# A branch prefetch hint at the head of each pass of the loops over row blocks in a three-layer graph network kernel

## The chip, the cores and the metric

The kernel runs on one core of one Trainium2 chip. The metric is the device time of one execution in microseconds; a kernel's time is the median of several executions.

## What is computed

`x` has 12,500 nodes of 64 features, `src` and `dst` list 412,500 edges. Three layers compute a gate for every edge and a gated, normalised sum over edges; a layer norm follows, then a plain degree-normalised sum with a dense product, and a second layer norm. Cut to what matters:

```python
for l in range(3):
    f1 = relu(x[row] @ nb_W[l] + nb_b[l]); f2 = relu(x[col] @ self_W[l] + self_b[l])
    h = relu(concatenate([f1, f2], axis=1) @ att1_W[l] + att1_b[l])
    mask = clip(sigmoid((h @ att2_W[l] + att2_b[l])[:, 0]) * 1.5 - 0.45, 0, 1)
    d = clip((segment_sum(mask, row) + 1e-6) ** -0.5, 0, 10)
    x = segment_sum((mask * d[row] * d[col])[:, None] * x[col], row)
    out = out + x
# then: layer norm; out = x + relu(segment_sum(x[col] * w, row) @ weight + bias); layer norm
```

## The kernel before

**Tiling.** The edges are sorted by row and column at the start (about the first 1.4 ms). Nodes form 98 blocks of 128 (`NB`), and all later edge work runs over the 98 blocks of rows, one after the other. Within a block of rows the edges lie in 51 tiles in 7 groups (`GROUPS`). Looking up `x[col]` and adding up per row are matrix products with one-hot matrices in fp8.

**Stages over row blocks.** There are seven such stages in an execution. Each of the three layers has an *edge stage*, which makes the gates (PE work: `cols` at L1033, `rows` at L1058, `row_sums` at L1083; in the first layer also `turn` at L1070, which transposes one-hots), and a *segment stage*, which sums the gated rows (PE work: `cols` at L1033, `scatter` at L1141). The seventh is the segment stage of the last graph layer. In the first edge stage DVE and ACT make the one-hots and SP stores them; in the others SP loads them.

**Engines.** Every engine (PE, DVE, ACT, POOL, SP) has its own instruction stream, and they meet only in semaphores. The order on each is the order in which it is written. A wait by `wait_alone` (L48) is an instruction of its own, EVENT_SEMAPHORE in the profile; L47 computes the value that it waits for, in a register.

**The loops.** A stage is written with `over_rows` (L415 and on): block 0 stands ahead of the loop in straight code, and a `Fori` of 97 passes does the other blocks. Its closing branch and its counter are recorded at L418, per pass one ALU_OP (counter + 1), one COMPARE_BRANCH (back to the head) and, at the head, one FUSED_REGOPS. PE, ACT and POOL use `over_rows` in all seven stages. DVE and SP use it in six: their part of the first edge stage is a `Fori` of its own, with 96 passes, outside `over_rows`. The stages of layers 2 and 3 stand once in the program, inside an outer loop over the layers.

Of the kernel before, what the change touches and what calls it, by code (L numbers as in the profile page):

```python
# [50 lines left out]
def gnn_kernel(nc, x, src, dst, nb_W, nb_b, self_W, self_b, att1_W, att1_b, att2_W, att2_b,  # L51
# [4 lines left out]
    NB = -(-N // P)  # L56
# [46 lines left out]
    with ExitStack() as ctx:  # L103
# [297 lines left out]
        def value(eng, e):  # L401
            return e if isinstance(e, int) else eng.snap(e)
# [12 lines left out]
        def over_rows(eng, t0, n0, body):  # L415

            body(value(eng, t0), value(eng, n0), 0, False)
            with eng.Fori(0, NB - 1) as i:  # L418
                body(eng.snap(t0 + 1 + i), eng.snap(n0 + 1 + i), eng.snap(i + 1), True)

        def over_slow(eng, n_slow, first, body):
# [6 lines left out]
        def _(sp):  # L428
# [108 lines left out]
            def edge_loads(layer):  # L537
                def rows_again(n, R):
                    wait_alone(sp, rs_ps, n + 1)
                    for i in range(3):  # L540
                        load_or(R, i)

                def block_of_rows(t, n, R, late):
                    if not late:
                        wait_alone(sp, z_ps, t * NG + NG)
                        wait_alone(sp, sc_ps, n * NG + NG)
                        for i in range(3):
                            load_oct(R, i)
                            load_ort(R, i)
                        return  # L550
                    for i in range(2):
                        wait_alone(sp, q_done, n * 3 + (i - 2))
                        load_oct(R, i)
                    wait_alone(sp, z_ps, t * NG + LAST[0])
                    load_ort(R, 0)
                    rows_again(sp.snap(n - 1), sp.snap(R - 1))
                    wait_alone(sp, q_done, n * 3)
                    load_oct(R, 2)
                    for i in range(1, 3):
                        wait_alone(sp, z_ps, t * NG + LAST[i])  # L560
                        load_ort(R, i)
                over_rows(sp, layer * (2 * NB), layer * NB, block_of_rows)
                rows_again(sp.snap(layer * NB + NB - 1), NB - 1)

            def segment_loads(t0, layer):
                def block_of_rows(t, m, R, late):
                    if not late:
                        wait_alone(sp, z_ps, t * NG + NG)
                        wait_alone(sp, sc_ps, m * NG + NG)
                        for i in range(3):  # L570
                            load_oct(R, i)
                        if not (isinstance(layer, int) and layer == L):
                            wait_alone(sp, rs_ps, layer * NB + NB + 1)
                        load_or(R, 0)
                        return
                    before = sp.snap(R - 1)
                    wait_alone(sp, sc_ps, m * NG + (LAST[1] - NG))
                    load_or(before, 1)
                    wait_alone(sp, z_ps, t * NG + LAST[0])
                    load_oct(R, 0)  # L580
                    wait_alone(sp, sc_ps, m * NG)
                    load_or(before, 2)
                    for i in range(1, 3):
                        wait_alone(sp, z_ps, t * NG + LAST[i])
                        load_oct(R, i)
                    wait_alone(sp, sc_ps, m * NG + LAST[0])
                    load_or(R, 0)
                over_rows(sp, t0, layer * NB, block_of_rows)
                m = layer * NB + NB
                for i in range(1, 3):  # L590
                    wait_alone(sp, sc_ps, value(sp, m * NG + (LAST[i] - NG)))
                    load_or(NB - 1, i)
# [55 lines left out]
        def _(pool):  # L648
# [64 lines left out]
            def gathers_for_edges(layer, first):  # L713
                def block_of_rows(t, n, R, late):
                    for k in range(XT):
                        gather_extra(t, k, q_d)
                    if not late and not first:
                        nc.gpsimd.tensor_tensor(total[:], total[:], x_cur[:], ALU.add).then_inc(total_added, 1)
                over_rows(pool, layer * (2 * NB), layer * NB, block_of_rows)
# [1204 lines left out]
```

## Time and profile before

| | |
|---|---|
| time, median of 3 executions | 11207.82 us (11200.24 to 11212.51) |
| the profiled execution's own time | 11290.33 us |
| its span, first to last instruction | 11288.6 us |
| busy: PE, PE weight loads, DVE, ACT, POOL | 79%, 70%, 72%, 28%, 39% |
| mean granted TensorE clock | 0.902 |

PE is TensorE's matmuls and PEld its weight loads; each matmul here has a weight load ahead of it in the same stream. A "q" behind an engine's name marks instructions that its sequencer handles alone (branches, register arithmetic, semaphore waits): they are not counted as busy, but the next instruction of that engine is dispatched behind them. The profiled execution is longer than the median by 82.5 us, and the rows below are all from it.

### The profile page before, as it was taken

The numbers are of one execution on the slowest core, as the hardware profiler recorded it, in microseconds if no ns is written. First come the engines' busy times: TensorE is split into PE (matmuls) and PEld (weight loads), VectorE is DVE, ScalarE is ACT, GpSimd is POOL, SyncE is SP. The second block draws the span as 40 slices with busy tenths as digits, with TensorE's granted clock in tenths as the row PEclk, the third lists the DMA queues.
The fourth block names the chain that finished last, engine by engine and source line by source line (L and its number), as shares of the span: only waits on it lengthen the run. The fifth ranks groups of instructions, "written<-read, shape, count | busy, mean of one in ns | idle before, by whom it ended". The sixth has DMA issues, their size and how long they took to land. (4 is left out here: it accounts for less than half of the span.)

```text
span 11288.6 us, 720231 instructions
## 1 busy us (share of the span) xinstructions
PE 8869.0 (79%) x288671; PEld 7908.7 (70%) x288671; DVE 8166.1 (72%) x13908; ACT 3160.3 (28%) x6110; POOL 4377.6 (39%) x4880
## 2 busy tenths in 40 slices
PE   0112288888888999888887999888888799969996
PEld 0112177777777888688886888688888688858885
DVE  9994477777777777666666777766666777777775
ACT  0110155555553333200002333300000333323332
POOL 0004300000016888111113777511111677758883
PEclk9655598999889999899998999999999999989997
DMA  1001266667655555465565555456655455545552
GB/s 24 0 0 26 63 204 205 207 211 211 205 180 147 152 152 152 138 175 174 173 174 146 151 150 151 123 173 175 174 172 174 136 151 151 150 109 152 151 152 74
DMA packets 1005300, 1633.48 MB, mean 145 GB/s; under 512 B 260438, under 2 KB 743634, under 8 KB 1004830
## 3 DMA queue, kind: packets, MB, share of 16 engines
q1 hardware_dynamic: 954104, 1581.29, 48.1%
q0 software_dynamic: 51104, 50.97, 2.3%
q8 instruction: 57, 0.93, 0.0%
q14 instruction: 35, 0.29, 0.0%
HBM read 1345.54 MB, written 286.24 MB: 145 GB/s over the span
## 5 line engine op out<-in xcount | busy, mean ns | idle before, releaser
L1033 PE MATMUL bank<-tab,extra 128*64 128x64 bf16 x201684 | 4306.9, 199 | 1023.4 <-issue 694.0
L1033 PEld LDWEIGHTS bank<-tab,extra 128*64 128x64 fp8e4 x201684 | 3779.3, 114 | 1622.7 <-issue 1559.0
L739 POOL TENSOR_TENSOR planes<-planes 128x448 f32<-128x448 f32 (+1 forms) x2744 | 2646.7, 965 | 732.8 <-DVE planes L1766 593.6
L888 ACT CAST bank<-planes 128x448 f32<-128x448 bf16 (+1 forms) x2744 | 1514.9, 552 | 2543.8 <-DVE planes L1759 1659.3
L669 POOL DMA_INDIRECT xg<-q_table,ixb x588 | 559.7, 952 | 4294.5 <-ACT ixb L837 4190.3
L1639 DVE SCALAR_TENSOR_TENSOR extra<-bank,a2w 128x448 f32<-128x448 f32 (+1 forms) x2058 | 1320.8, 642 | 1158.1 <-PE bank L1058 960.0
L1141 PE MATMUL bank<-planes,extra 128*128 128x192 bf16 x19992 | 2104.2, 247 | 27.0 <-POOL planes L739 9.0
L1759 DVE TENSOR_TENSOR planes<-bank,mask_all 128x448 f32<-128x448 f32 (+2 forms) x2744 | 1710.6, 623 | 425.8 <-PE bank L1033 270.2
L1766 DVE TENSOR_TENSOR planes<-planes,bank 128x448 f32<-128x448 f32 (+1 forms) x2744 | 1729.2, 630 | 126.4 <-ACT bank L888 126.3
L1058 PE MATMUL bank<-plb,extra 128*128 128x64 bf16 x44982 | 1692.7, 198 | 14.1 <-ACT plb L869 9.5
L1141 PEld LDWEIGHTS bank<-planes,extra 128*128 128x128 fp8e4 x19992 | 1576.8, 96 | 142.2 <-issue 25.0
L1058 PEld LDWEIGHTS bank<-plb,extra 128*128 128x128 fp8e4 x44982 | 1520.4, 101 | 67.7 <-issue 15.0
L1646 DVE TENSOR_REDUCE lg<-extra 128x7 f32<-128x448 f32 (+1 forms) x2058 | 1267.0, 628 | 0.1
L669 POOL DMA_INDIRECT xg<-xd_table,ixb x784 | 760.1, 970 | 394.5 <-issue 188.1
L865 ACT CAST extra<-bank 128x512 fp8e4<-128x512 f32 (+2 forms) x1470 | 702.2, 524 | 649.6 <-PE bank L1070 637.1
L869 ACT COPY plb<-planes 128x192 bf16 (+1 forms) x294 | 103.3, 351 | 2211.0 <-PE bank L1058 2200.4
L1655 DVE TENSOR_SCALAR extra<-work,iota_p 128x2944 fp8e4<-128x2944 uint8 (+2 forms) x490 | 665.2, 1358 | 3.8 <-DVEq L48 3.6
L950 PE MATMUL bank<-ident,tab 128*128 128x128 f32 x224 | 41.1, 369 | 675.4 <-DVE tab L1296 675.4
L1070 PE MATMUL bank<-total,extra 128*128 128x128 bf16 x4998 | 503.1, 233 | 64.5 <-ACT extra L865 48.7
L950 PEld LDWEIGHTS bank<-ident,tab 128*128 128x128 f32 x224 | 39.5, 200 | 677.4 <-issue 343.6
L1083 PE MATMUL bank<-mk,extra 128*128 128x4 bf16 x14994 | 428.9, 165 | 15.2 <-DVE mk L1623 14.3
L1070 PEld LDWEIGHTS bank<-total,extra 128*128 128x128 fp8e4 x4998 | 327.5, 104 | 153.9 <-issue 76.9
(227 smaller groups left out, 4427.1 us busy)
## 6 DMA issues: line engine op xcount, KB each, us to landing
extra<-one_hots SPq DMA_DIRECT2D x1372, 368.0 KB, 3.2
extra<-one_hots SPq DMA_DIRECT2D x2156, 224.0 KB, 3.5
extra<-one_hots SPq DMA_DIRECT2D x588, 192.0 KB
one_hots<-extra SPq DMA_DIRECT2D x490, 224.0 KB, 2.0
one_hots<-extra SPq DMA_DIRECT2D x294, 368.0 KB, 3.6
work<-slot_rows_cols SPq DMA_DIRECT2D x196, 368.0 KB, 4.9
work<-slot_rows_cols SPq DMA_DIRECT2D x294, 224.0 KB, 3.8
work<-slot_rows_cols SPq DMA_DIRECT2D x98, 192.0 KB
```

Of the source, the lines that this page charges most:

```text
L669: nc.gpsimd.indirect_dma_start(out=to, out_offset=None, in_=table_d, in_offset=bass.IndirectOffsetOnAxis(ap=index, axis=0)).then_inc(done, 16)
L739: nc.gpsimd.tensor_tensor(tiles(yrl[:, 2, a * C:b * C]), tiles(yrl[:, 1, a * C:b * C]), upper[:, 1, a:b, :], ALU.subtract).then_inc(low_re ...
L865: nc.scalar.copy(orr[:, k * P:(k + n) * P], turn_to(j)[:, 0:n * P], saturate=False).then_inc(or_made, 1)
L888: nc.scalar.copy(tiles(z_banks[g][:, 0:(b - a) * C]), upper[:, 0, a:b, :]).then_inc(high_ps, 1)
L1033: mm = pe.matmul(bank[half * S:(half + 1) * S, i * C:(i + 1) * C], oct_[:, k * P + half * S:k * P + (half + 1) * S], tab[:, at:at + C], st ...
L1058: mm = pe.matmul(bank[:, i * C:(i + 1) * C], ort[:, k * P:(k + 1) * P], plb[:, pl * C:(pl + 1) * C], start=False, stop=True, skip_group_ch ...
L1070: mm = pe.matmul(turn_to(j)[:, i * P:(i + 1) * P], ort[:, (k + i) * P:(k + i + 1) * P], ident_bf, start=True, stop=True, skip_group_check= ...
L1141: mm = pe.matmul(sum_bank[:, 0:NPL * C], orr[:, k * P:(k + 1) * P], upper[:, :, k, :], start=(k == 0), stop=(k == TT - 1))
L1639: v.scalar_tensor_tensor(tiles(yv[g % 3][:, 0:w]), tiles(bank_of(g, first)[:, 0:w]), 0.0, a2w[:].unsqueeze(1).to_broadcast([P, w // C, C]) ...
L1646: v.tensor_reduce(lg[:, k0:k1], tiles(yv[g % 3][:, 0:(k1 - k0) * C]), AX_X, ALU.add).then_inc(lg_done, 1)
L1759: v.tensor_tensor(tiles(yrl[:, 0, a * C:at * C]), tiles(z_banks[g][:, 0:(at - a) * C]), mask_all[:, bass.ds(R * TT + a, at - a)].unsqueeze ...
L1766: v.tensor_tensor(yrl[:, 1, a * C:b * C], yrl[:, 0, a * C:b * C], z_banks[g][:, 0:(b - a) * C], ALU.subtract).then_inc(z_used, 1)
```

## The change

Each engine's loop in `over_rows` gets a branch prefetch hint for its own closing branch. It is the first instruction of every pass; nothing else in the pass changes. Loops outside `over_rows` are as before.

```diff
         def over_rows(eng, t0, n0, body):
 
             body(value(eng, t0), value(eng, n0), 0, False)
-            with eng.Fori(0, NB - 1) as i:
+            with nc.Fori(0, NB - 1, engines=(eng.engine,), hint_back_edge=True) as i:
                 body(eng.snap(t0 + 1 + i), eng.snap(n0 + 1 + i), eng.snap(i + 1), True)
```

On PE, at the head of the loop of the first edge stage, the instructions of the changed kernel stand against those of before like this (`UNCONDITIONAL_BRANCH` enters the loop from block 0; the loop's first instruction is the one behind it; ISA at L418 is the FUSED_REGOPS of the profile):

```order
 L1070 MATMUL bank<-total,extra 128x128 x9
 L418 UNCONDITIONAL_BRANCH
+L418 BRANCH_PREFETCH_HINT
 L418 ISA
 L47 ISA
```

One instruction has been put ahead of the register work; nothing has changed its place. The same on PE at the head of the loop of the edge stages of layers 2 and 3:

```order
 L1058 MATMUL bank<-plb,extra 128x64 x63
 L418 UNCONDITIONAL_BRANCH
+L418 BRANCH_PREFETCH_HINT
 L418 ISA
 L47 ISA
```

Again one instruction more at the head and none moved. DVE, ACT, POOL and SP get the same single instruction at the head of each of their `over_rows` loops.

## Rows read from the trace of the kernel before

**Rows 1.** The page: busy time of each engine, and its instruction queues.

```profile
PE 8869.0 (79%) x288671; PEld 7908.7 (70%) x288671; DVE 8166.1 (72%) x13908; ACT 3160.3 (28%) x6110; POOL 4377.6 (39%) x4880
...
q8 instruction: 57, 0.93, 0.0%
q14 instruction: 35, 0.29, 0.0%
```

**Rows 2.** Windows in three loops: PE, PEld, DVE, ACT, POOL busy; clock, DMA share.

```profile
1440.00:3360.00 1920.00, 1661.10 (x52261) 1497.35 (x52256) 1502.56 (x2474) 1087.39 (x1905) 182.04 (x190) 0.90 0.67 206
3450.00:4500.00 1050.00, 995.41 (x32280) 868.41 (x32279) 800.59 (x1406) 379.42 (x748) 842.95 (x937) 1.00 0.55 152
4670.00:6040.00 1370.00, 1207.58 (x46601) 1127.96 (x46602) 897.47 (x1968) 82.84 (x282) 178.20 (x188) 0.93 0.60 173
```

**Rows 3.** DMA queues (packets, MB, share), 1380 to 1430 us: entering first loop.

```profile
q1 hardware_dynamic: 5198, 9.95, 62.5%
q8 instruction: 9, 0.15, 1.4%
q0 software_dynamic: 96, 0.10, 1.2%
q14 instruction: 3, 0.02, 0.2%
```

**Rows 4.** DMA queues, all there are, 1440 to 3360 us: inside first loop.

```profile
q1 hardware_dynamic: 204423, 389.26, 64.9%
q0 software_dynamic: 6080, 6.24, 2.2%
issues: line engine op xcount, KB each, median us to landing
```

**Rows 5.** DMA queues, all there are, 4670 to 6040 us: second edge loop.

```profile
q1 hardware_dynamic: 121180, 231.28, 57.7%
q0 software_dynamic: 6016, 6.17, 2.0%
```

**Rows 6.** All of L418: engine op xcount, ns min/median/max, first and last start.

```profile
L418 PEldq FUSED_REGOPS  x679: 56/59/133, 1408.0 to 11115.2; - x170
...
L418 PEldq ALU_OP  x679: 32/32/32, 1430.0 to 11126.0; - x170
L418 PEldq COMPARE_BRANCH  x679: 76/208/248, 1430.1 to 11126.1; - x170
...
L418 ACTq COMPARE_BRANCH  x679: 40/45/50, 1430.4 to 11127.3; - x170
...
L418 DVEq COMPARE_BRANCH  x582: 50/56/78, 3446.1 to 11127.9; - x194
```

**Rows 7.** PE, one head, edge stage of layer 2: weight loads, then sequencer instructions.

```profile
5415.90 1.67 PEld L1058 LDWEIGHTS bank<-plb,extra 128*128 128x128 fp8e4 x55
5417.87 1.22 PEld L1033 LDWEIGHTS bank<-tab,extra 128*64 128x64 fp8e4 x71 [0.29 <-issue]
...
L418 PEldq ALU_OP  x1: 32/32/32, 5417.0 to 5417.0; - x1
L418 PEldq COMPARE_BRANCH  x1: 207/207/207, 5417.1 to 5417.1; - x1
...
L48 PEldq EVENT_SEMAPHORE  x2: 51/51/51, 5417.6 to 5417.8; - x2
...
L47 PEldq FUSED_REGOPS  x1: 46/46/46, 5417.7 to 5417.7; - x1
```

**Rows 8.** PE, one head of the first edge stage, likewise.

```profile
2519.87 0.13 PEld L1070 LDWEIGHTS bank<-total,extra 128*128 128x128 fp8e4 x2 [0.64 <-issue]
2520.72 1.38 PEld L1033 LDWEIGHTS bank<-tab,extra 128*64 128x64 fp8e4 x81 [0.72 <-issue]
...
L48 PEldq EVENT_SEMAPHORE  x2: 51/51/51, 2520.4 to 2520.6; - x2
```

**Rows 9.** PE, segment stage: head at 4242.14; at 4240.84 and 4243.72 no branch.

```profile
4240.84 0.55 PEld L1033 LDWEIGHTS bank<-tab,extra 128*64 128x64 fp8e4 x30 [0.16 <-issue]
4241.44 0.54 PEld L1141 LDWEIGHTS bank<-planes,extra 128*128 128x128 fp8e4 x7
4242.14 0.84 PEld L1033 LDWEIGHTS bank<-tab,extra 128*64 128x64 fp8e4 x48 [0.16 <-issue]
...
4243.72 0.84 PEld L1033 LDWEIGHTS bank<-tab,extra 128*64 128x64 fp8e4 x48 [0.16 <-issue]
...
L48 PEldq EVENT_SEMAPHORE  x2: 51/51/51, 4241.7 to 4241.9; - x2
```

**Rows 10.** Waits inside the second edge stage (4670 to 6040): us, times, longest.

```profile
ACT plb L869 <- PE bank L1058: 1064.2, 94, 12.9
DVE extra L1639 <- PE bank L1058: 351.5, 372, 2.2
```

**Rows 11.** PE in the loop's first pass: a stretch of code not yet there.

```profile
1413.58 0.41 PE L1033 MATMUL bank<-tab,extra 128*64 128x64 bf16 x14 [2.70 <-issue]
```

## The prediction

> **What bounds the kernel now.** I read the page first, for who is busy: PE leads with 79% of the span, DVE follows with 72% [rows 1]. Then the busy time by stretch, since the change sits in seven loops that make up most of the time. In the segment loop PE is busy 995 of 1050 us and DVE 801, in the edge loop of layer 2 PE 1208 of 1370 and DVE 897, in the first edge loop PE 1661 of 1920 and DVE 1503 [rows 2]. The waits of the layer-2 edge loop say the same from the other side: DVE stands idle for PE 351.5 us and ACT 1064.2 us [rows 10], so PE is what they follow. In all seven loops I take PE as the engine whose delay becomes the stage's delay.
>
> The hint is meant for a loop whose head has to be fetched again at each closing branch. So the third view is the DMA queues, where instruction fetches have queues of their own. Over the whole execution q8 carries 57 packets, 0.93 MB, thus 16 KB each, and q14 35 packets [rows 1]. While block 0 and the first pass of the first loop run (1380 to 1430 us), q8 has 9 packets and q14 has 3 [rows 3]. Inside that loop, 1440 to 3360 us, some 95 passes, neither queue moves one packet [rows 4]; the same in the edge loop of layer 2 [rows 5]. All code of a pass stays resident, although PE's pass has some 550 matmuls (52261 over 95 passes, [rows 2]) and as many weight loads. There is no fetch at the closing branch that a hint could bring forward. What a fetch that comes late looks like stands in the first pass: PE idle 2.70 us on "issue" [rows 11]. At the later heads nothing of that size is seen: PE's weight loads pause 0.29 us in the layer-2 edge loop [rows 7], 0.72 us in the first edge loop [rows 8] and 0.16 us in the segment loop [rows 9].
>
> The Trainium skill, "Runtime: NRT & Kernel Launch", section "Instruction fetch mechanics", says that a taken branch whose target isn't in the current 2-page window forces a fetch before execution goes on, with pages of 256 instructions; it speaks for the hint, and with over 1,000 PE instructions in a pass it would have one fetch at each head. This trace doesn't agree: zero instruction packets in 1920 us. The same section gives TensorE room for 2048 instructions, and with that figure the trace agrees.
>
> **The change, part by part.** *What it adds:* one sequencer instruction at each head. PE has 679 heads reached through L418's register work, DVE 582 [rows 6]; ACT and POOL as PE, SP as DVE. *What it removes:* nothing that these rows show. *What it moves:* nothing.
>
> *Its price on PE.* No row shows a hint. The nearest are PE's other sequencer instructions: ALU_OP 32 ns, EVENT_SEMAPHORE 51, FUSED_REGOPS 59, and the taken branch 208 [rows 6, 7]. In the profile a place in the stream costs more than its record: from the wait at 5417.6 over a FUSED_REGOPS at 5417.7 to the wait at 5417.8 it is 0.1 us from each to the next, for records of 51 and 46 ns [rows 7]. Half of that is between records. The profiled execution is 82.5 us longer than the median of the others, and PE's heads of the three edge loops have six such instructions each: 3 x 97 x 6 x 0.05 us = 87 us. So I take the time between records to be the recorder's for the larger part, and the hint at 0.05 us without it, at 0.1 us in the profile. Bounds: 0.032 us (ALU_OP's record) and 0.117 us (0.1 us slot, with FUSED_REGOPS' 59 ns in place of 46 and rounding).
>
> *What of it is on the path.* This depends on what ends PE's pause at the head.
> - Edge loops of layers 2 and 3: the last wait is at 5417.8 and the first weight load at 5417.87 [rows 7]: the load goes right behind the sequencer, the array has run dry, and anything put into the sequence delays it in full. 2 x 97 heads.
> - First edge loop: last wait at 2520.6, load at 2520.72 [rows 8]: the same. 97 heads. No wait there lasts longer than its 51 ns, so no other engine hides it.
> - Four segment loops: the pause at the head is 0.16 us, and just 0.16 us also where the same kinds of instructions follow each other with no branch between (4240.84, 4243.72). The last wait is at 4241.9, the load at 4242.14, 0.24 us later against 0.07 in rows 7 [rows 9]. So the sequencer is ahead there by 0.13 to 0.17 us, and a hint of up to 0.117 us disappears. The cover is the seven scatter matmuls, which the array is still working off; if it were gone, the four loops would cost 4 x 97 x 0.05 = 19 us more.
>
> *The other engines.* DVE, ACT, POOL and SP pay a similar 0.05 to 0.1 us per pass. DVE waits for PE 351.5/94 = 3.7 us per pass in the edge loop, ACT 11 us [rows 10]; in the segment loop DVE and POOL have 249 and 207 us free over 93 passes, more than 2 us a pass [rows 2]. I count them at nothing. Without that slack DVE alone would cost 582 x 0.1 = 58 us.
>
> *The sum.* 3 x 97 = 291 exposed heads. At 0.05 us: +14.6 us. Low bound 0.032: +9 us. High bound 0.117: +34 us. On the profiled execution at 0.1 us a head: 11290.3 + 29 = 11319 us. The median of the other executions before is 11207.8; with 14.6 us it becomes **11222.4 us**, +0.13%. A measurement of this kernel can tell about 0.2%, 22 us, from no change. The hint crosses that line from 0.077 us a head.
>
> **The rivals.**
> 1. *Slower, plainly: the hint starts a fetch although the target is resident.* Then each PE pass brings one 16 KB packet on q8, 679 more. The packet alone costs nothing visible (DMA share 0.55 to 0.67, [rows 2]). If it displaces code of the same pass, that has to come again, and PE waits as in [rows 11]: up to 679 x 2.70 = 1830 us, 13,040 us in all. A hint that takes a taken branch's price in the sequencer belongs here too: with 0.2 us exposed on 291 heads and some 0.06 us past the cover on 388, +58 + 23 = 81 us, 11,289 us. For it: nothing shows what the hint does with a resident target. Against it: a request for what is there has no work to do. It decides from a price of 0.077 us, and in the large form from the first displaced block.
> 2. *Faster: the hint makes the taken branch cheap.* PE's branch takes 208 ns taken and 76 at the least, presumably where it isn't taken; ACT's and DVE's take 45 and 56 when taken [rows 6]. If PE's 132 ns are a look-up that the hint does in advance, 291 exposed heads give back 38 us and cost 15: 11,184 us, -0.2%. Against it: the target is fixed and resident, and the hint comes a whole pass earlier.
> 3. *Faster by a hidden fetch.* If there were fetches in the loops that the queues don't show, the most they can give back is all of PE's pauses at the heads: 97 x 0.72 + 194 x 0.29 + 388 x 0.16 = 188 us, 11,020 us. The rule of the Trainium skill above ("Instruction fetch mechanics") is the case for it. Against it: the queues do show fetches in between the loops, with the sizes of whole blocks, and in the pauses all time is filled by six recorded instructions.
> 4. *The change does nothing that can be measured:* the sequencer's delay is swallowed in the exposed loops too, or the hint is dropped from the program: 11,208 us.
>
> **How the numbers follow.** Forecast (a small price on PE's exposed heads): 0.78, of which 0.52 stay under 22 us and 0.26 exceed it, as the price may be that of the profile. Rival 1: 0.07. Rival 2: 0.06, on the line, counted as faster 0.05. Rival 3: 0.02. Rival 4: 0.07. So faster 0.07, same 0.60, slower 0.33. The range for 8 in 10: from 11,200 us (rival 4 with the measurement's own spread, the lowest run before being 11,200.2) to 11,255 us (the high bound, 34 us, with some of the segment heads uncovered, 388 x 0.03 = 12 us). It leaves out rivals 2 and 3 and the larger half of rival 1.
>
> **What would show it.** In the profile after: 679 BRANCH_PREFETCH_HINT at L418 on PE with a record between 30 and 60 ns; no instruction packets inside the loops, and 57 and 35 (give or take two) in all; PE's branch still 208 ns; the pause ahead of the first weight load 0.29 to about 0.39 us in the edge loops of layers 2 and 3 and 0.72 to about 0.82 in the first; still 0.16 in the segment loops. I am wrong if q8 has hundreds of packets (rival 1), if the branch shortens (rival 2), if the segment loops lengthen too (the cover is thinner than I read it), or if another engine's head proves to set a pass.

## The result, and the profile after

The changed kernel takes 11277.43 us (median of 4 executions, 11271.08 to 11283.9), the kernel before 11207.4 us (4 executions). The ratio is 1.0063, with a 95% interval of 1.0051 to 1.0076: **slower by 0.63%, 70 us**. Forecast were 11,222 us within 11,200 to 11,255, with 0.33 for slower.

The page after, the lines that answer to [rows 1]:

```profile
PE 8841.6 (78%) x288671; PEld 7878.9 (70%) x288671; DVE 8165.3 (72%) x13908; ACT 3160.0 (28%) x6110; POOL 4377.1 (39%) x4880
...
q8 instruction: 57, 0.93, 0.0%
q14 instruction: 34, 0.28, 0.0%
```

All instructions recorded at L418 (duration min/median/max in ns, first and last start), against [rows 6]:

```profile
L418 PEldq BRANCH_PREFETCH_HINT  x679: 35/35/59, 1399.7 to 11095.5; - x170
...
L418 PEldq COMPARE_BRANCH  x679: 80/216/259, 1423.0 to 11106.5; - x170
...
L418 ACTq COMPARE_BRANCH  x679: 44/49/73, 1423.3 to 11107.6; - x170
...
L418 DVEq BRANCH_PREFETCH_HINT  x582: 39/39/61, 3399.9 to 11097.2; - x194
...
L418 DVEq COMPARE_BRANCH  x582: 55/61/94, 3412.7 to 11108.3; - x194
```

The DMA queues inside the edge loop of layer 2 (4650 to 6030 us), against [rows 5]:

```profile
q1 hardware_dynamic: 121774, 232.50, 57.0%
q0 software_dynamic: 6055, 6.21, 1.9%
```

So the hint is there 679 times on PE, and neither instruction queue has a packet in this stretch, as before. The median of the branch became longer, not shorter, by 8 ns on PE and by 4 to 5 ns on ACT and DVE.

PE's weight loads after, at a head of the edge loop of layer 2 (against [rows 7]), at one of the first edge loop (against [rows 8]) and around one of a segment loop, the one at 4067.28 (against [rows 9]); the last row is the semaphore waits at this segment head:

```profile
5361.46 2.29 PEld L1033 LDWEIGHTS bank<-tab,extra 128*64 128x64 fp8e4 x138 [0.39 <-issue]
```

```profile
2520.68 2.39 PEld L1033 LDWEIGHTS bank<-tab,extra 128*64 128x64 fp8e4 x138 [0.78 <-issue]
```

```profile
4065.94 0.55 PEld L1033 LDWEIGHTS bank<-tab,extra 128*64 128x64 fp8e4 x30 [0.16 <-issue]
4066.53 0.54 PEld L1141 LDWEIGHTS bank<-planes,extra 128*128 128x128 fp8e4 x7
4067.28 0.87 PEld L1033 LDWEIGHTS bank<-tab,extra 128*64 128x64 fp8e4 x48 [0.20 <-issue]
...
4068.89 0.84 PEld L1033 LDWEIGHTS bank<-tab,extra 128*64 128x64 fp8e4 x48 [0.16 <-issue]
```

```profile
L48 PEldq EVENT_SEMAPHORE  x2: 51/51/51, 4066.9 to 4067.2; - x2
```

The pause of layer 2's edge head went from 0.29 to 0.39 us, a full 0.1 us. The segment head's pause went from 0.16 to 0.20, while the pauses beside it, with no branch in them, stayed at 0.16. Before, the weight load there came 0.24 us behind the last wait; now it comes 0.08 us behind it (4067.2, 4067.28): the cover is gone.

### The profile page after: what moved, and what is told of

Same layout as the page of the kernel before. It is cut to its first block and busy times, and to the rows that moved or that the text cites. A ratio compares the mean times of both kernels' runs of the same rounds, so it can differ in the third digit from the quotient of the medians.

```text
span 11269.3 us, 723432 instructions
## 1 busy us (share of the span) xinstructions
PE 8841.6 (78%) x288671; PEld 7878.9 (70%) x288671; DVE 8165.3 (72%) x13908; ACT 3160.0 (28%) x6110; POOL 4377.1 (39%) x4880
## 5 line engine op out<-in xcount | busy, mean ns | idle before, releaser
L1058 PE MATMUL bank<-plb,extra 128*128 128x64 bf16 x44982 | 1682.5, 198 | 14.7 <-ACT plb L869 10.6
L1083 PE MATMUL bank<-mk,extra 128*128 128x4 bf16 x14994 | 427.5, 165 | 21.3 <-DVE mk L1623 14.2
L1083 PEld LDWEIGHTS bank<-mk,extra 128*128 128x128 fp8e4 x14994 | 411.3, 98 | 31.1 <-issue 21.6
```

The costliest lines, as they stand in the source:

```text
L1058: mm = pe.matmul(bank[:, i * C:(i + 1) * C], ort[:, k * P:(k + 1) * P], plb[:, pl * C:(pl + 1) * C], start=False, stop=True, skip_group_ch ...
L1083: mm = pe.matmul(sum_bank[:, 0:NPL + 1], orr[:, k * P:(k + 1) * P], mk_upper[:, k, :], start=(k == 0), stop=(k == TT - 1), skip_group_chec ...
```

## The experiments

The runs fell on five chips, and each ratio is against the kernel before on the same chip. That matters here: before takes 11,289 us on the first chip (e1 to e4), 11,211 on the third (e9 to e12), and 10,215 to 10,218 on the other three. From here on, the first and the third are called the slower chips, the others the quick ones.

| run | what carries the change | before, us | this, us | ratio, 95% |
|---|---|---|---|---|
| e1 | nothing (the kernel before) | 11289.26 | 11285.85 | 1.0 [0.9991, 1.0009] |
| e2 | hint on PE alone | 11289.26 | 11346.94 | 1.0045 [1.0032, 1.0059] |
| e3 | hint on the four others | 11289.26 | 11288.65 | 0.9998 [0.9989, 1.0007] |
| e4 | another instruction, PE | 11289.26 | 11330.87 | 1.0036 [1.0023, 1.005] |
| e5 | the whole change | 10217.54 | 10251.18 | 1.0032 [1.002, 1.0044] |
| e6 | PE, edge loops | 10217.54 | 10234.81 | 1.0018 [1.0009, 1.0027] |
| e7 | PE, segment loops | 10217.54 | 10224.15 | 1.0007 [0.9998, 1.0016] |
| e8 | no hint, a wait moved | 10217.54 | 10181.83 | 0.9966 [0.9952, 0.9979] |
| e9 | no hint, aligned heads, PE | 11211.17 | 11215.0 | 1.0001 [0.9992, 1.001] |
| e10 | aligned heads and hint, PE | 11211.17 | 11266.78 | 1.005 [1.0036, 1.0064] |
| e11 | two blocks a pass | 11211.17 | 12664.85 | 1.1298 [1.1282, 1.1314] |
| e12 | two blocks a pass, hint | 11211.17 | 12521.51 | 1.1173 [1.1158, 1.1189] |
| e13 | as e6 | 10216.04 | 10226.45 | 1.0012 [1.0003, 1.0021] |
| e14 | as e7 | 10216.04 | 10224.21 | 1.0008 [0.9999, 1.0017] |
| e15 | a wait moved, hint on PE | 10216.04 | 10206.01 | 0.9988 [0.9979, 0.9997] |
| e16 | as e8 | 10216.04 | 10180.42 | 0.9966 [0.9954, 0.9978] |
| e17 | as e6 | 10215.26 | 10236.85 | 1.0021 [1.0012, 1.003] |
| e18 | as e7 | 10215.26 | 10222.07 | 1.0008 [0.9999, 1.0017] |

### Which engine pays, and is it the hint: e1 to e4

```diff
-            with eng.Fori(0, NB - 1) as i:
+            with nc.Fori(0, NB - 1, engines=(eng.engine,), hint_back_edge=eng.engine == mybir.EngineType.PE) as i:
```

e3 has `!=` in place of `==`. e4 has no hint, but an instruction that does nothing at the head of PE's loops: `eng.nop(nofuse=True)` ahead of `body`.

> The kernel before, unchanged, for a second profile on the same chip as the other kernels of this group. Its ratio to itself should be 1.000 within 0.001; its profile should show whether the 11290 us of the first profiled execution (82 us over the median of the others) is usual for a profiled execution or one odd one. If it is usual, the new profile is again near 11290 us; if it was odd, near 11207 us, with the difference in the first edge loop, whose passes took 20.17 us on average there.

> The hint on PE alone. Theory A, the cost is PE's sequencer time at the head: nearly all of the 70 us, ratio 1.005 to 1.007. Theory B, the cost comes from the heads of the other engines (DVE first): near 1.000 to 1.001 here. Theory C, many small parts: in between.

> The hint on DVE, ACT, POOL and SP, not on PE. Theory A: ratio 1.000, within 0.001. Theory B: 1.005 to 1.007. If this and the run with PE alone add up to 1.0063, the costs are independent.

> No hint; in its place PE's sequencer runs one NOP at the head of each pass. If a hint costs only the time of one more sequencer instruction (and its shift of the code behind it by one place), this is as slow as the run with the hint on PE alone, within 0.001. If the hint has a price of its own in the fetch logic, this is near 1.001 and the other well above it.

Measured: e1 and e3 nothing, e2 +58 us, e4 +42 us, with overlapping intervals. On this chip PE alone carries the effect. Between e2 and e4 lie 16 us, and the five executions of each hardly overlap (the slowest of e4 took 11333.9 us, the quickest of e2 11333.3), so the other instruction explains most of the hint's price, but not all. The rows of e4 at L418 on PE, and one of its heads in the edge loop of layer 2:

```profile
L418 PEldq MOVE  x686: 29/29/38, 1405.9 to 11140.5; - x172
...
L418 PEldq COMPARE_BRANCH  x679: 76/208/248, 1428.1 to 11151.5; - x170
```

```profile
5252.26 2.29 PEld L1033 LDWEIGHTS bank<-tab,extra 128*64 128x64 fp8e4 x138 [0.40 <-issue]
```

The profile has no record of a NOP. What it shows is one recorded instruction more at e4's head: a MOVE of 29 ns (686, of which 7 stand ahead of the loops in e1 and e9 too), with the counter's register work behind it as a FUSED_REGOPS of L47 in place of that of L418. The pause here is 0.40 us, as long as with the hint. So in this loop plain register work costs about what the hint costs: it is a place in PE's sequence. The 8 ns on the branch aren't surely the hint's own either: e9 and e16, without any hint, have branches of 215 ns too.

Where the time went is read from PE's closing branches: the first and the last start in a loop give its length over 96 passes. The edge loop of layer 2 in e1, then in e2, with the window of each (busy PE, PEld, DVE, ACT, POOL; clock, DMA share, GB/s):

```profile
L418 PEldq COMPARE_BRANCH  x97: 76/208/218, 4649.6 to 6053.0; - x97
4640.00:6060.00 1420.00, 1247.91 (x48177) 1166.09 (x48177) 930.59 (x2037) 84.93 (x289) 186.32 (x197) 0.93 0.59 172
```

```profile
L418 PEldq COMPARE_BRANCH  x97: 80/216/227, 4670.0 to 6087.6; - x97
4660.00:6090.00 1430.00, 1257.05 (x48115) 1175.26 (x48115) 928.41 (x2030) 84.56 (x288) 182.61 (x193) 0.92 0.59 171
```

1403.4 us became 1417.6, thus 14.2 us or 0.148 us a pass, where the head grew by 0.102. PE's busy time grew too, with no more matmuls, and the granted clock of the window went from 0.93 to 0.92. The passes themselves show where this comes from. Two of e1, from branch to branch:

```profile
4677.70:4691.70 14.00, 12.23 (x503) 11.41 (x500) 9.56 (x22) 0.88 (x3) 1.90 (x2) 1.00 0.60 182
4691.70:4707.90 16.20, 14.46 (x507) 13.59 (x503) 9.66 (x23) 0.88 (x3) 1.90 (x2) 0.79 0.61 180
```

The passes of this loop are of these two kinds: about 14.0 us with the clock granted in full (2.4 GHz), or 16.2 us where a part of the pass runs at the lower level (0.5 in the records, 1.2 GHz). Each long pass of e1 has such a part, no short one does. By the records of e1 and e2, the short passes grew by 0.055 us each, thus 5 us, and the long ones went from 27 to 31 of the 96 (26 to 32 in the same loop of layer 3), thus 9 us (12 in layer 3). e4 has 31 in both loops. So more than half of the loop's growth is passes at the lower clock, and less than half is the head. Without the hint on PE the profiles on chips of this time have 26 to 29 (29 twice in e3), so the step to 31 and 32 is small, but e9 to e10 shows it again: 23 to 29 and 23 to 27. Why the clock falls more often isn't shown.

### Which loops pay: e5 to e8

```diff
-                over_rows(pe, layer * (2 * NB), layer * NB, first_block_of_rows if first else block_of_rows)
+                over_rows(pe, layer * (2 * NB), layer * NB, first_block_of_rows if first else block_of_rows, hint=True)
```

e6 is this: PE's hint in the three edge loops alone. e7 does the same at the call of the segment loops, e5 is the changed kernel whole. e8 has no hint; in the edge stages PE's wait for `z_used` of the next block's first group, which stood at the head, stands in the pass before, and the register work that computes its value goes with it, two instructions in all:

```diff
                     for g in range(NG):
+                        if g == NG - 2:
+                            wait_alone(pe, z_used, value(pe, t * NG + NG + 1))
                         rows(n, g)
...
-                else:
+                elif not (g == 0 and waited[0]):
                     wait_alone(pe, z_used, t * NG + g + 1)
```

> The whole change once more, in one group with the next three. Expected: PE alone gave 1.0045 and the other engines 0.9998, so about 1.0045 to 1.0063. Its mean granted clock should lie below that of the kernel before, as it did with the hint on PE alone (0.898 to 0.900 against 0.900 to 0.905), if the longer pause in the edge stages has a part in the clock.

> The hint on PE alone and in the three edge stages alone. There the pause at the head grew from 388 to 490 ns, the slot of one hint. Theory A1, slot alone: 291 heads x 0.102 us = 30 us, ratio 1.0026. Theory A2, slot plus more time at the low clock level because of the longer pauses: 1.0035 to 1.0045, and a mean granted clock about 0.003 lower than before's.

> The hint on PE alone and in the four segment stages alone. As predicted before the result (the array's backlog covers it): 1.000. By the profile after, where the pause at the head grew from 258 to 285 to 299 ns: 388 x 0.03 = 12 us, 1.001. The granted clock stays that of before.

> No hint. PE's wait for z_used of group 0 of the next pass, with the register work for it, is moved from the head of the edge stages' loops to a place ahead of the matmuls of group 5 of the pass before, where the sequencer runs ahead. If each sequencer instruction at an exposed head costs its slot of about 0.1 us, in either direction, the pause shrinks by 0.1 to 0.2 us on 291 heads: 29 to 58 us less and ratio 0.995 to 0.9975, with the granted clock slightly up. If the pause is set by something else, 1.000.

Measured on this quicker chip: the whole change +34 us, edges +17, segments +7 (its interval reaches to nothing). The two parts make 24 us, not 34, and where the other 10 lie isn't shown. e6's 17 us is below the 30 that 291 heads at 0.102 us would give. The expected fall of the mean granted clock didn't come: it is 0.93 in both, as in before. e8 is faster than both kernels, by 36 us against before: two instructions fewer at the edge heads give twice what one more costs in e6.

### Is it where the code lies: e9 and e10

`Fori` can place the loop's first instruction at a chosen place within a fetch block; e9 does this on PE and has no hint, e10 has the hint too.

```diff
-            with eng.Fori(0, NB - 1) as i:
+            with nc.Fori(0, NB - 1, engines=(eng.engine,), head_slot={mybir.EngineType.PE: 0} if eng.engine == mybir.EngineType.PE else None) as i:
```

> No hint. On PE the first instruction of each of the loops over row blocks is loaded at the start of a fetch block; nothing else changes. Theory P, place of code matters: the pause at the heads of the segment loops of layers 2 and 3, or its period, differs from before by some 0.05 to 0.1 us, as it did when hints in other loops moved the code; ratio 0.998 to 1.002. Theory N, place does not matter: 1.000 and periods as before.

> As the kernel with aligned loop heads, and the hint on PE in all seven stages. Against that kernel only the hint and the shift of the body by one place are new. If the segment loops' extra pause comes from the hint's slot, it is 0.03 us or more again there and the whole is 0.002 to 0.0045 above the aligned kernel; if it came from where the code lay, the segment loops are as in the aligned kernel and only the edge stages' 0.1 us a head remain, 0.002 to 0.003.

e9 is level, e10 is 52 us above it. The place of the head doesn't make the cost, and aligning doesn't remove it. It does move the pause: over the edge heads of layers 2 and 3 the median distance from load to load is 0.44 us in e9 against 0.39 in e1, and 0.49 to 0.50 in e10. The hint's share of the pause is thus 0.05 to 0.06 us here and 0.10 in e1 to e2, at nearly the same price in time.

### A loop that doesn't stay resident: e11 and e12

PE's edge loops do two blocks of rows per pass, 48 passes and one block behind them. e12 has the hint on these loops.

```diff
+            if two:
+                with nc.Fori(0, NB // 2 - 1, engines=(eng.engine,), hint_back_edge=False) as i:
+                    body(eng.snap(t0 + 1 + i * 2), eng.snap(n0 + 1 + i * 2), eng.snap(i * 2 + 1), True)
+                    body(eng.snap(t0 + 2 + i * 2), eng.snap(n0 + 2 + i * 2), eng.snap(i * 2 + 2), True)
+                body(value(eng, t0 + NB - 1), value(eng, n0 + NB - 1), NB - 1, True)
+                return
```

> No hint. In the edge stages PE's loop does two blocks of rows in a pass (48 passes, the last block in straight code), so that its body has over 2,050 instructions, about double. If all code of a pass of before stays resident because it is small enough, this body should no longer fit: instruction packets on q8 in every pass, and the closing branch followed by a pause of 1 to 3 us, against 0.39 before; the time then rises by 3 x 48 x 1 to 3 us = 140 to 430 us, less what the halved heads give back (3 x 48 x 0.35 = 50 us). If code of any length is kept, no packets and 50 us less.

> As the kernel with two blocks of rows in a pass of PE's edge loops, and the hint on those loops. If that body does not fit, the hint has something to bring forward: the pause behind the closing branch should fall from 1 to 3 us to about 0.5, and the time by 100 us or more against the same kernel without it. If the hint does nothing useful even then, the two are alike, this one 0.1 us a pass slower.

The pages' instruction queue and PE's closing branches in the edge loop of layer 2 (in e11 the first 46 of the 48), of e11 and then of e12:

```profile
q8 instruction: 1493, 24.46, 0.8%
...
L419 PEldq COMPARE_BRANCH  x46: 3457/3977/5117, 5064.2 to 6853.4; - x46
```

```profile
q8 instruction: 1401, 22.95, 0.7%
...
L419 PEldq COMPARE_BRANCH  x48: 88/2201/3381, 5051.3 to 6846.9; - x48
```

With some 1,000 matmuls and as many weight loads in a pass, q8 carries (1493 - 57) / 144 = 10 packets a pass and the branch takes 4 us. There the hint does what it is for: the branch falls to 2.2 us, though not to the 0.5 expected, and the kernel gets 143 us faster. Both are still 12 to 13% slower than the kernel before. Expected of e11 were 140 to 430 us more; it took 1454 more, of which the branches' medians explain 144 x (3.98 - 0.21) = 543. Its mean granted clock is 0.859, that of e9 0.909; the rest was not traced further. The Trainium skill, "Runtime: NRT & Kernel Launch", section "Instruction fetch mechanics", gives TensorE room for 2048 instructions and says that a taken branch whose target lies outside the current 2-page window forces a fetch. The room agrees with these two cases (48177 / 97 = 497 matmuls and as many weight loads in one block's pass bring no packets, twice that and the sequencer's instructions bring 10); the 2-page window doesn't, since 994 instructions are almost four pages of 256.

### What stayed open, tried again: e13 to e18

e13 and e17 are e6, e14 and e18 are e7, e16 is e8. e15 is e8 with the hint on PE.

> Hint on PE in the three edge loops alone, the same kernel as the earlier edges run, to see it where PE's passes hold the 0.72 us pauses. If the price is the head's alone, 291 x 0.102 = 30 us. If the longer head also costs clock, 40 to 50 us and a larger share of low clock in the edge loops.

> Hint on PE in the four segment loops alone. If the hint overruns the cover there by 0.03 to 0.04 us a head, 388 x 0.035 = 14 us. If the cover held as predicted, 0. If the two parts add up, this and the edges run make the 50 to 70 us of the whole change.

> Hint on PE and the head's wait of the edge loops moved into the pass before. If what counts is the number of sequencer instructions between branch and first weight load, the hint takes back what the moved wait gives in the edge loops and costs 14 us in the segment loops: 10 to 30 us above before. If the hint's price has another cause (a fetch, a look-up), the moved wait and the hint still add, so this run can't be above the early run by less than 50 us either way; by the first theory it is 45 to 60 us above it.

> No hint; the head's wait of the edge loops on PE is moved into the pass before, as in the earlier run of it, which gave 36 us on a quicker chip. By the sequencer theory two instructions fewer at 291 heads give 40 to 60 us on a chip with low clock in the edge loops, 30 to 40 on one without. If the gain was that chip's alone, nothing.

> Hint on PE in the three edge loops alone. Of use where the chip's before is near 11,200 us, for which no run of this kernel stands yet: the head's price alone gives 291 x 0.102 = 30 us, with clock lost in the edge loops 40 to 50 us. Where before is near 10,217 us it repeats 10 to 17 us.

> Hint on PE in the four segment loops alone. Where the chip's before is near 11,200 us: 388 x 0.035 = 14 us by the overrun of the cover alone; 25 us or more if the rest of the 70 us is here. Where before is near 10,217 us it repeats 7 to 8 us.

All six fell on chips where before takes 10,216 us. Over the three such chips edges alone cost 17, 10 and 22 us, segments alone 7, 8 and 7. e16 repeats the gain of 36 us. e15 is 26 us above e16, less than the 45 to 60 expected, and 10 us below before, where 10 to 30 above it were expected: the edges' price is smaller on these chips, as it was without the moved wait. The heads of layer 2's edge loop in e14 (neither), e16 (wait moved; the load starts at 4894.80, the group before it ends at 4892.81 + 1.89, thus 0.10 us) and e15 (wait moved and hint):

```profile
4900.98 2.29 PEld L1033 LDWEIGHTS bank<-tab,extra 128*64 128x64 fp8e4 x138 [0.29 <-issue]
```

```profile
4892.81 1.89 PEld L1059 LDWEIGHTS bank<-plb,extra 128*128 128x128 fp8e4 x63
4894.80 2.29 PEld L1034 LDWEIGHTS bank<-tab,extra 128*64 128x64 fp8e4 x138
```

```profile
4904.60 2.29 PEld L1034 LDWEIGHTS bank<-tab,extra 128*64 128x64 fp8e4 x138 [0.20 <-issue]
```

Two instructions fewer at the head (behind the branch e16 has one FUSED_REGOPS and one wait, e14 two of each) take 0.29 to 0.10, one more takes 0.10 to 0.20: about 0.1 us each, and moved wait and hint add. Layer 2's edge loop in e16, then in e15:

```profile
L418 PEldq COMPARE_BRANCH  x97: 83/215/218, 4297.1 to 5421.1; - x97
4290.00:5425.00 1135.00, 1129.66 (x48078) 1078.03 (x48070) 902.16 (x2031) 84.76 (x289) 183.60 (x195) 1.00 0.72 215
```

```profile
L418 PEldq COMPARE_BRANCH  x97: 80/221/240, 4300.0 to 5436.8; - x97
4295.00:5440.00 1145.00, 1131.38 (x48022) 1078.28 (x48017) 908.79 (x2029) 84.57 (x288) 183.00 (x193) 1.00 0.72 213
```

Here the hint costs 12.8 us or 0.133 us a pass; PE's busy time hardly moves, and the clock is 1.00 in both.

The first edge loop in e14 (no hint there) and in e13 (with it):

```profile
L418 PEldq COMPARE_BRANCH  x97: 76/208/252, 1316.5 to 3073.3; - x97
```

```profile
L418 PEldq COMPARE_BRANCH  x97: 80/216/254, 1319.2 to 3069.2; - x97
```

1756.8 us without and 1750.0 with the hint: in this pair it costs nothing in this loop. The moved wait says the same from the other side: it shortened the pause at these heads from 0.70 us (e14) to 0.47 (e16), and the loop took 1757.4 us. So the pause at the head doesn't set the pass there, and the whole gain of e16 lies in the edge loops of layers 2 and 3, 21.1 and 19.6 us shorter than in e14.

## Why the prediction failed, step by step

The same reading in every loop (for e9 and e10 without the branch recorded at the loop's entry, which these two kernels have besides), as the change in its length from one kernel to the other on the same chip, in us. Each is one profile against one. The row of e3 is the yardstick: its PE program is that of e1, and its lengths still differ by up to 8 us.

| | first edge | edge 2 | edge 3 | the four segment loops |
|---|---|---|---|---|
| e1 to e2 | +12.8 | +14.2 | +17.4 | +6.2, -2.9, -2.8, +9.1 |
| e1 to e4 | -5.0 | +13.4 | +15.8 | +1.7, +5.8, +5.0, +1.9 |
| e1 to e3 | +3.3 | +5.7 | +7.6 | -1.0, -4.7, -4.1, -0.7 |
| e9 to e10 | -7.6 | +15.7 | +11.7 | +3.3, +4.5, +4.8, +6.8 |
| e16 to e15 | -3.9 | +12.8 | +10.6 | +6.9, -6.3, -6.5, +5.3 |

- **The step that failed: the sum, 291 heads x 0.05 us and nothing else.** The price was half of what it is, the segment heads stood at nothing, and a longer pause at a head was taken to cost its own length and no more. With the price at 0.102 us and the segment heads at 0.03 the sum comes to 29.7 + 12 = 42 us, or 11,249 us, still inside my range; the result lies 28 us above that. What such a sum has no term for shows on the first chip: about 20 us of more passes at the lower clock in the edge loops of layers 2 and 3, and 16 us outside the loops, in two profiles that are 70 us apart (the medians 58). The points that follow take the terms one by one.
- **The price, 0.05 us, the rest "the recorder's".** I found that a place in the stream takes 0.1 us in the profile, and halved it because the profiled execution was 82.5 us longer than the median. Those two numbers are most likely of different chips: 11290.33 fits the first chip, where before takes 11289.26, and 11207.8 fits the third, with 11211.17. On one chip the profiled execution isn't the longer one: in e1 it took 11276.83 us against a median of 11285.85, in the kernel after 11271.08 against 11277.43. So nothing was to be taken off. The head of layer 2's edge loop grew by 0.102 us, by the medians of e1 and e2: 0.093 from the hint to the next instruction, and 8 ns on the branch. The pause moved from 0.29 to 0.39 as I had said for the profile; I had only refused to believe it for the time.
- **Which heads are exposed.** I counted 291 alike, at the pause's price. The edge loops of layers 2 and 3 pay more than their 96 x 0.102 = 9.8 us each: 10.6 and 12.8 us with the clock at 1.00 (e16 to e15), 12 to 18 us on the slower chips, where there are more passes at the lower clock. The first edge loop has the longer pause (0.78 us after), yet its length fell in two of the hint's three pairs and from e14 to e13 too, and grew in one; so the hint costs nothing sure there. That the load goes right behind the sequencer shows that the pause is the sequencer's; it doesn't show that the pause sets the pass, and e16 shows that there it doesn't. What sets that pass is not settled. 194 heads at 0.102 us make 20 us, near the 17, 10 and 22 that the edges alone cost on the quick chips.
- **The cover of the segment heads.** I had them ahead by 0.13 to 0.17 us and the hint within that. On the slower chips the cover was used up: median distance from load to load over the head, worked out from the records, went from 258 ns (e1) to 294, 274, 285 and 294 (e2). So my fallback case, "some uncovered", was the rule there, at 0.03 us a head: 388 x 0.03 = 12 us. On a quick chip the cover nearly held (e14: 279, 262, 259 and 259 ns). The loops' lengths give 9.6, 19.4 and -0.6 us for the hint's three pairs, and the times of e7, e14 and e18 are 7 to 8 us up. The two signs within a pair (e2, e15) are larger than what the head explains, and repeat; they stay unexplained. The row of e3, with no hint on PE, has up to 4.7 us in these loops, and e10, with aligned heads, has one sign only.
- **The other engines at nothing:** right on the chip where it was tried (e3, 0.9998).
- **No fetch in the loops, nothing to bring forward:** right, down to 57 packets on q8 in the whole execution. Rivals 1 (fetch), 3 and 4 are out. Rival 1's other form, a price of 0.2 us on the exposed heads, has the right size of result, but not the mechanism: the slot is 0.1. Rival 2 had the branch getting cheaper; it got 8 ns dearer.
- **The sum.** On the slower chips: edge loops 2 and 3 give 31.6 and 27.4 us, the segment loops 9.6 and 19.4, the first edge loop +12.8 and -7.6, together 54.0 and 39.1. The profiled executions differ by 70.1 (e1, e2) and 56.3 us (e9, e10), so 16 to 17 us more lie outside the loops. In e9 to e10, 7.5 of the 17 lie ahead of the first closing branch and behind the last, where one hint runs at most, so that much is the spread of two profiles. In e1 to e2 it lies between the loops, in pieces of 0.6 to 4.2 us. From e1 to e4 only 0.2 us lie outside the loops, so this part may be the hint's own, and it is as much as e2 and e4 differ by in the whole kernel; but that rests on one pair of profiles, and I have no cause for it. The result's 70 us is above the 58 and 52 us of e2 and e10; no split run is known to be from its chip, and where the difference lies is open.

**What is shown and what is argued.** Shown: PE alone carries the cost (e2, e3, on one chip); one other instruction in its place costs 42 us of the 58 (e4); two instructions fewer at the head give time back (e8, e16), all of it in the edge loops of layers 2 and 3; inside the loops no fetch is involved, and where one is, the hint helps (e12). Shown by the passes of one profile each: that on the slower chips more than half of the surplus in the edge loops of layers 2 and 3 is passes at the lower clock. Not shown: why there are more of them, what the hint costs outside the loops, and why at clock 1.00 the price was still 12.8 / 96 = 0.133 us a pass, above the 0.102 of the head.

**The version that beats both** is e8: 10181.83 against 10217.54 us before and 10251.18 us with the change. Per pass of layer 2's edge loop its repetition e16 takes 11.71 us (1124.0 / 96), where e14, without hint there, takes 11.93 (1145.1 / 96, its branches run from 4303.6 to 5448.7). It was run on two quick chips; on a slower one it wasn't tried.

## What to carry to other kernels

Look at the instruction queues inside a loop before asking for a prefetch: with no packets there, a hint is one more sequencer instruction at the worst place, behind the branch, and its price on PE is about a whole slot of 0.1 us on each head that the array has run dry at and that sets the pass. A long pause at a head isn't enough to say so: ask whether the loop gets shorter when the pause does. The gain lies in the other direction: take waits and register work from the head into the middle of the pass, where matmuls are queued. Where the clock isn't granted in full, sort the passes by length first: a mean over both kinds hides what the head costs. And don't discount a duration of the trace on the strength of a difference between two runs, unless they are known to be of one chip.

## What the runs showed of the hardware that I had not expected

The chips differ by up to 10% on one and the same program, and half of the difference has a place: the edge loops of layers 2 and 3 make 514 of the 1050 us between the profiles of e1 and e14. In the edge loop of layer 2 on the chip of [rows 7], PE's weight loads pause three times in the middle of a pass, with nothing in the trace that they wait for, and nearly twice as long as at the head:

```profile
5403.86 2.29 PEld L1033 LDWEIGHTS bank<-tab,extra 128*64 128x64 fp8e4 x138 [0.33 <-issue]
...
5408.14 0.14 PEld L1033 LDWEIGHTS bank<-tab,extra 128*64 128x64 fp8e4 x2 [0.56 <-issue]
5408.89 0.14 PEld L1033 LDWEIGHTS bank<-tab,extra 128*64 128x64 fp8e4 x3 [0.61 <-issue]
5409.67 0.19 PEld L1033 LDWEIGHTS bank<-tab,extra 128*64 128x64 fp8e4 x6 [0.63 <-issue]
```

On a quick chip (e14) the same stretch has none. Behind the head at 4900.98 (shown above) all runs through to the next head:

```profile
4903.32 0.76 PEld L1058 LDWEIGHTS bank<-plb,extra 128*128 128x128 fp8e4 x24
4904.12 0.74 PEld L1033 LDWEIGHTS bank<-tab,extra 128*64 128x64 fp8e4 x42
...
4912.91 2.20 PEld L1033 LDWEIGHTS bank<-tab,extra 128*64 128x64 fp8e4 x133 [0.29 <-issue]
```

The pass is 11.93 us there (4912.91 - 4900.98) and 14.01 here (5417.87 in [rows 7] less 5403.86), with a clock of 0.99 to 1.00 against 0.93 over the whole loop. The clock isn't what makes a short pass longer: e1's pass of 14.00 us has it at 1.00 too. What makes these pauses isn't known; in these loops they are larger than anything that this change gave or took. A taken branch to a head that isn't resident costs PE 4 us (e11), 19 times the 208 ns of a resident one.
